# Band matrices made whole, statistics row by row, squares in longer pieces and fewer filler matmuls in a two-branch image kernel

## The reference

```python
def reference(x, ln_w, ln_b, q_w, q_dw, kv_w, kv_dw, proj_w, temperature, w1, w3, w5, wd, wf):
    x = x + attention(_gn(x), ...)       # L0
    x = x + convolutions(_gn(x), ...)    # L1
    return x

def _gn(v, G=32, eps=1e-05):             # group norm, 3 channels a group, no weights
    g = v.reshape(B_, G, C_ // G, H_, W_)
    m = jnp.mean(g, axis=(2, 3, 4), keepdims=True)
    s = jnp.var(g, axis=(2, 3, 4), keepdims=True)
    return ((g - m) / jnp.sqrt(s + eps)).reshape(v.shape)

# attention: xn = layer norm over channels; q = dwconv3x3(conv1x1(xn, q_w), q_dw); kv likewise;
#   k, v = split(kv); q, k normed along the pixels; softmax(q k^T * temperature) v; conv1x1(., proj_w)
# convolutions: x1 = 1x1, x2 = 3x3, x3 = 5x5, x4 = 3x3 dilated by 2; conv1x1(concat(x1..x4), wf)
```

## Time and profile before

| | us |
|---|---|
| median of 3 runs (lowest, highest) | 1850.2 (1848.76, 1851.78) |
| the profiled execution: its time | 1848.9 |
| its span | 1847.2 |
| PE busy | 1754.8 (95%) |
| DVE busy | 1517.0 (82%) |
| ACT busy | 1024.4 (55%) |
| POOL busy | 516.1 (28%) |

### The profile page before, as it was taken

One profiled execution on the slowest core, in us unless ns is written; L12 is line 12 of the kernel. 1 busy time (PEld: TensorE's weight loads), 2 busy tenths in 40 slices (PEclk: granted clock), 3 DMA queues, 4 the chain that ended last, 5 costly groups with the idle time before them and its releaser, 6 DMA issues.

```text
span 1847.2 us, 43054 instructions
## 1 busy us (share of the span) xinstructions
PE 1754.8 (95%) x14228; PEld 1678.0 (91%) x14228; DVE 1517.0 (82%) x2182; ACT 1024.4 (55%) x1736; POOL 516.1 (28%) x347
## 2 busy tenths in 40 slices
PE   4999999999999999999999999999999999999998
PEld 3889878999989996999999997889998999699998
DVE  4799868999877657999968665899996865689997
ACT  0756556555285746655437663755536665665451
POOL 5599500232272000123238000022325400003222
PEclk9999989999999998999999999899999999899999
DMA  7012203566501200566630210166661121035553
GB/s 192 0 35 68 63 1 78 149 173 169 159 18 51 75 11 1 122 168 177 171 107 13 68 55 1 36 156 167 175 165 44 36 71 30 1 81 153 131 143 99
DMA packets 101476, 166.83 MB, mean 90 GB/s; under 512 B 40040, under 2 KB 74568, under 8 KB 101224
## 3 DMA queue, kind: packets, MB, share of 16 engines
q1 hardware_dynamic: 76040, 136.91, 29.3%
q10 hardware_dynamic: 25344, 28.75, 4.8%
HBM read 52.86 MB, written 25.17 MB: 42 GB/s over the span
## 4 chain that ended last, share of the span: by engine, by line
PE 73%; issue 8%; DVE 7%; ACT 4%; DMA 2%; POOL 1%; ACTq 1%; SPq 1%; DVEq 1%; POOLq 0%
PE ps L802 35%; PE ps L661 11%; PE ps L704 6%; PE ps L680 6%; PE ps L682 6%; PE ps L681 6%; DVE region L1208 3%; ACT region L948 2%; PE ps L635 2%; DMA X<-in_x_dram 1%; POOL region L560 1%; PE ps L797 1%; PE ps L733 1%; DMA region<-region 1%; PE ps L691 0%
## 5 line engine op out<-in xcount | busy, mean ns | idle before, releaser
L802 PE MATMUL ps<-region,W 128*96 128x256 f16 (+4 forms) x7156 | 803.9, 272 | 10.9 <-ACT region L976 10.5
L802 PEld LDWEIGHTS ps<-region,W 128*96 128x96 f16 (+2 forms) x7156 | 781.2, 122 | 25.1 <-issue 19.6
L570 POOL TENSOR_TENSOR region<-region 96x528 f32<-96x528 f32 (+1 forms) x72 | 96.4, 1344 | 1013.1 <-ACT region L962 689.4
L1208 DVE TENSOR_TENSOR region<-V,band 128x387 f32<-128x387 f32 (+2 forms) x288 | 298.3, 1098 | 82.9 <-PE ps L682 81.4
L981 ACT ACTIVATE region<-region 96x1584 f16<-96x1584 f32 (+2 forms) x88 | 110.8, 1301 | 329.6 <-DVE region L1298 308.5
L680 PE MATMUL ps<-region 128*128 x1152 | 225.7, 278 | 9.4 <-DVE region L1208 8.8
L682 PE MATMUL ps<-region 128*128 x1152 | 222.7, 275 | 0.0
L681 PE MATMUL ps<-region 128*128 x1152 | 222.2, 274 | 0.0
L1384 DVE SCALAR_TENSOR_TENSOR region<-ps,small,region 96x768 f32<-96x768 f32 (+1 forms) x220 | 203.7, 988 | 14.2 <-PE ps L802 12.9
L661 PE MATMUL ps<-proj,region 96*128 96x240 f32 x1024 | 212.9, 372 | 0.0
L661 PEld LDWEIGHTS ps<-proj,region 96*128 96x128 f32 x1024 | 197.9, 194 | 14.0
(11 more groups left out here) (169 smaller groups left out, 2170.7 us busy)
## 6 DMA issues: line engine op xcount, KB each, us to landing
region<-region SPq DMA_DIRECT2D x108, 247.5 KB, 4.0
region<-in_x_dram SPq DMA_DIRECT2D x128, 192.0 KB, 2.4
out_dram<-region SPq DMA_DIRECT2D x40, 576.0 KB, 4.2
region<-region ACTq DMA_DIRECT2D x80, 247.5 KB, 2.4
X<-in_x_dram SPq DMA_DIRECT2D x30, 576.0 KB, 6.0
region<-region SPq DMA_DIRECT2D x36, 247.4 KB, 4.9
X<-in_x_dram SPq DMA_DIRECT2D x19, 384.0 KB, 14.8
region<-region SPq DMA_DIRECT2D x24, 185.6 KB, 3.6
```

The source lines that it names most:

```text
L802: last = mm(o, w, src, start=k == 0, stop=k == len(steps) - 1, skip_group_check=split and ck > 0)
L1208: v.tensor_tensor(T[:, i, 3 * c:3 * c + m].rearrange("p m (i j) -> p m i j", j=3), taps.broadcast_to([P, m, BW // 3, 3]), mask.broadcast_t ...
```

## The change

There are four edits.

- *Band matrices.* From the second chunk of each image on, one operation of 2322 elements makes a chunk's 18 matrices and raises `s_T` by 3. The first chunk keeps its three operations. The first pair of chunks stands ahead of the loop, which now begins at the second pair.
- *First image's statistics.* Each of the 16 loads has a semaphore of its own. DVE's 32 `bn_stats` are written out without a loop, each load's two behind a wait for that load: 12 loads ahead of the search for the largest weight, two behind line 1107, one behind line 1111, the last behind line 1119 and ahead of the seven scalings.
- *Squares.* Seven sets are squared in one piece of 2048 each, in a loop; the last set follows outside the loop in two pieces of 1024. There is one scratch buffer, and every piece waits until the one before it has finished.
- *Fillers.* 40 instead of 64 filler products ahead of unit 0.

```diff
-        tsums = sb("tsums", [C, AT + AT // 2])
+        tsums = sb("tsums", [C, AT + AT // 4 + 1])
...
-        junk = [work[0:C, a:a + BANK].bitcast(bf16) for a in (900, 900 + BANK)]
+        junk = work[0:C, 900:900 + 2 * BANK].bitcast(bf16)
...
-        s_first = [plain_sem("first_rows_loaded%d" % k) for k in range(LS // UG)]
+        s_first = [plain_sem("first_rows_loaded%d" % k) for k in range(LS)]
...
-                keep_warm(0, 64)
+                keep_warm(0, 40)
...
-                with act.Fori(0, SETS) as k:
+                def squared(k, half, parts, n):
+                    width = 4 * BANK // parts
+                    act.wait_ge(s_xs, b * (SETS + 1) + n + START)
+                    act.activation(junk[:, 0:width], X[:, bass.ds(k * 4 * BANK + half * width, width)], ACT.Square,
+                                   bias=col(MEAN), scale=-1.0, accum_out=tsums[:, bass.ds(AT + n, 1)]).then_inc(s_xs, 1)
+                with act.Fori(0, SETS - 1) as k:
                     act.wait_ge(s_x1, (b * SETS + k + 1) * AR + START)
-                    for u in range(2):
-                        act.wait_ge(s_xs, (b * SETS + k) * 2 + u - 1 + START)
-                        act.activation(junk[u], X[:, bass.ds((k * 2 + u) * 2 * BANK, 2 * BANK)], ACT.Square,
-                                       bias=col(MEAN), scale=-1.0,
-                                       accum_out=tsums[:, bass.ds(AT + k * 2 + u, 1)]).then_inc(s_xs, 1)
+                    squared(k, 0, 1, k)
+                act.wait_ge(s_x1, (b + 1) * SETS * AR + START)
+                for half in range(2):
+                    squared(SETS - 1, half, 2, SETS - 1 + half)
...
+            def statistics(first, end):
+                for m in range(first, end):
+                    dve.wait_ge(s_first[m], 16)
+                    for t in range(m * XL, m * XL + XL):
+                        v.bn_stats(stats[:, t, :], X[:, t * BANK:(t + 1) * BANK]).then_inc(s_bn, 1)
+            statistics(0, 12)
...
-                with dve.Fori(0, DK // 2) as k2:
+                def bands(k2, i, parts):
...
+                    for c, channels in parts:
+                        m = 3 * channels
+                        taps = V[:, :, bass.ds((k2 * 2 + i) * DM + 3 * c, m)].rearrange("p j m -> p m j").unsqueeze(2)
+                        v.tensor_tensor(T[:, i, 3 * c:3 * c + m].rearrange("p m (i j) -> p m i j", j=3),
+                                        taps.broadcast_to([P, m, BW // 3, 3]), mask.broadcast_to([P, m, BW // 3, 3]),
+                                        ALU.mult).then_inc(s_T, len(PARTS_OF_T) // len(parts))
+                WHOLE = ((0, DC),)
+                bands(0, 0, PARTS_OF_T)
+                bands(0, 1, WHOLE)
+                with dve.Fori(1, DK // 2) as k2:
                     for i in range(2):
...
+                        bands(k2, i, WHOLE)
```

More of the change, by code:

```diff
@@ L372, in _ @@
                 sync.dma_start(X[:, m * LR * W:(m + 1) * LR * W],
-                               x[0:1, :, m * LR:(m + 1) * LR, :].rearrange("o c h w -> (o c) (h w)")).then_inc(s_first[m // UG], 16)
+                               x[0:1, :, m * LR:(m + 1) * LR, :].rearrange("o c h w -> (o c) (h w)")).then_inc(s_first[m], 16)
             def stage_rows(b, c, j, free):
@@ L1108, in _ @@
             assert setup.n == N_AMAX
+            statistics(12, 14)
             dve.wait_ge(s_pt, 15)
@@ L1112, in _ @@
             assert setup.n == N_GMAX
+            statistics(14, 15)
             dve.wait_ge(s_pt, 16)
@@ L1120, in _ @@
             assert setup.n == N_WSC
+            statistics(15, LS)
             for at, factor in OSCS:
                 link(setup, v.tensor_scalar(col(at), col(POW), factor / (WTOP * YSCALE), None, ALU.mult))
-            first_statistics(LS // UG - 1)
             NEXT_AT = 500
@@ L1194, in _ @@
                     scaled(AT - AD + i, i, i == AD - 1)
-                with dve.Fori(0, DK // 2) as k2:
-                    for i in range(2):
[L1200 to L1210, removed]
+                def bands(k2, i, parts):
+                    n = b * DK + k2 * 2 + i
+                    dve.wait_ge(s_dw, n - 1 + START)
+                    dve.wait_ge(s_out, b * UNITS * 16 + START)
+                    dve.wait_ge(s_pq, (b + 1) * AT + START)
+                    dve.wait_ge(s_V, N_TURNED)
+                    mask = band[:].rearrange("p (i j) -> p i j", j=3).unsqueeze(1)
+                    for c, channels in parts:
[8 more added lines that the diff above has]
+                with dve.Fori(1, DK // 2) as k2:
+                    for i in range(2):
+                        bands(k2, i, WHOLE)
                 dve.wait_ge(s_qd, (b + 1) * DK + START)
@@ L1261, in _ @@
                 assert st.n == N_MEAN2
-                dve.wait_ge(s_xs, (b + 1) * AT // 2 + START)
+                dve.wait_ge(s_xs, (b + 1) * (SETS + 1) + START)
                 squares_of(st, tsums)
```

## The result

| | before | after |
|---|---|---|
| median of 9 runs of each, side by side (lowest, highest) | 1850.15 (1848.1, 1852.5) | 1842.18 (1838.92, 1846.11) |
| the profiled execution: its time | 1848.9 | 1841.69 |

A forecast was written before the change was run, and what follows sets the result against it. PE bounds the depthwise stage, except in the first image, where DVE and POOL take turns at the port; ACT's chain sets the seams. Terms -9.2 + 0.5 + 0.9 - 1.4 + 0.6 + 0 = -8.6 gave 1841.6 us; range 1838 to 1847.

The forecast's parts named there:

- Band matrices, -9.2: First image's depthwise stage: one operation meets at most one POOL turn, so PE becomes the bound; 9.2 us less, bounds 4 and 10.2.
- Only part comes back: Rival: turns fall badly and leftovers hold up the first image's Gram stage; 1846 to 1848 us, chance 0.13.
- Second chunk, +0.3: Depthwise stage, images 2 to 4: whole operation exposes handover and slower first matmul; 0.3 us more an image, 0.9 in all.
- POOL's leftovers, +0.5: First image's Gram stage: 8 to 12 POOL operations move there and meet DVE's copies; 0.5 us more, bounds 0 and 3.
- Statistics, -1.4: First image's setup: DVE keeps up with the loads, so ACT's folding and PE's 24 filler records start earlier; 1.4 us less.
- a case that the prediction named: Setup: if the cold clock holds for longer in the 24 filler records, the statistics give only 1.1 us.
- Squares, +0.6: Last set of squares: second piece waits for the first's accumulator; 0.15 us more an image, bounds -0.1 and +0.3.
- Fillers, 0: Ahead of unit 0: it starts 3.6 us earlier, but unit 1 still waits for ACT's last copy; 0 us in all.
- the slower rival: Units 0 and 1: fewer fillers bring clock drops, 1.5 to 1.7 us lost at each; 1855 us, chance 0.04.
- the sign that I had named: Wait for ACT's last copy grows from 10.5 to about 17 us; if it stays or goes, the prediction is wrong.

## Why the prediction was right

*Band matrices, -9.2: right, measured -9.06 with the stage's start.* PE became the bound, as the sum had it. The mechanism was confirmed from the other side too: with POOL silent the old operations give 97.10. The mean wait for a turn was 0.50 (0.36 against an undisturbed operation), where I took 0.65 and "at most one turn"; the turn of 2.43 was worked out to 0.03. The Trainium skill (SBUF — State Buffer, "SBUF: two separate sides") is borne out by the operation at 123.48.

*Only part comes back* (the first rival) is out: the first image's depthwise stretch is 98.7, within 1.5 of the others'.

*Second chunk, +0.3: right in size, by two numbers.* The stage itself is 0.43 longer; its first product comes 0.11 earlier, since the first chunks now stand outside the loop (argued, not shown). The copy of the second chunk came 4.44 after that of the first, 567.51 against 563.07, instead of 576.93 - 572.91 = 4.02. With three parts for the second chunk again the 0.43 vanished.

*POOL's leftovers, +0.5: the mechanism right, the size too small.* I had 8 to 12 operations in the Gram stage with the question open whether one-input copies wait for POOL. 15 remained, and POOL's split ended at 233.51, 21 us behind the depthwise stretch's end instead of 8 to 12, perhaps because DVE's wider operations also hold POOL back for longer (argued, not shown). And the copies do wait: 1215 ns instead of 993, as this timeline shows (DVE, then POOL):

```profile
228.19 1.01 DVE L1225 COPY region<-region 128x960 f32 x1 [0.69 <-PE ps L704]
230.09 1.54 DVE L1225 COPY region<-region 128x960 f32 x1 [0.88 <-PE ps L704]
231.99 3.15 DVE L1225 COPY region<-region 128x960 f32 x2 [0.35 <-PE ps L704]
...
228.28 2.44 POOL L522 TENSOR_TENSOR W<-region,W 96x768 f16<-96x768 f32 x1
230.78 2.73 POOL L538 MEMSET W<- 128x2208 f16 x1
```

The copy of 228.19 began 0.09 ahead of POOL's L522 and took 1.01, no longer than with POOL silent, and L522 ended 1.52 after it. That of 230.09 met the end of L522 and took 1.54. The two of 231.99, met by a memset that reads nothing, took 3.15 together. The term is 1.03 at full clock, within its bounds of 0 and 3.

*Statistics, -1.4: right in kind, too large.* 1.18 and 0.41 in the pairs with nearly equal landing. The first pair of profiles read 1.65, with the last rows landed 43.40 - 42.38 = 1.02 later in the kernel before. What I had not allowed for is this scatter. The lower value goes with longer fillers (5.38 for the 24 records), a case that the prediction named but took for -1.1. That it is the clock is not shown.

*Squares, +0.6: wrong, measured -0.04 an image.* The later second piece (+0.12) was as forecast. I took the gain of leaving the loop as "up to 0.1"; it was 0.17, the start 0.12 instead of 0.29 behind the end of DVE's last addition.

*Fillers, 0: right for the path to unit 1, not shown for the whole time.* Unit 0 started 3.4 earlier (forecast 3.6), except in the third image, whose fillers had run at full clock before (14.54 for all 128 records instead of 16.17). PE stood 3.38, 1.77 and 2.02 ahead of it in the first three images, where I had 1.7. The gain was gone by unit 1. Alone, the edit came out 3 us slower, and no trace ties that to the fillers. The wait for ACT's last copy grew from 10.5 to 12.0, not to 17: the rest stands in the waits for DMAs, 12.4 in total, because unit 0's third point waits too, and because 3.4 us at or near 1.2 GHz at unit 0's start eat a part:

```profile
285.40:289.00 3.60, 0.77 (x6) 0.75 (x7) 3.53 (x4) 0.17 (x1) 0.00 (x0) 0.95 0.65 142
289.00:292.40 3.40, 3.40 (x19) 3.19 (x18) 2.69 (x2) 3.40 (x3) 0.00 (x0) 0.55 0.21 43
292.40:295.80 3.40, 3.40 (x33) 3.40 (x32) 3.21 (x4) 3.40 (x3) 0.00 (x0) 1.00 0.12 28
```

PE did 0.77 of work in 3.60, and then 19 products in 3.40 instead of 33. This is the clock drop that the slower rival named; the price per drop was right, and the wait behind it hides it: unit 1 starts 0.06 later than before, counted from the group mean. With the fillers changed alone the wait for ACT's last copy was 10.2 and that for DMAs 15.4, while unit 1 stayed where it was. So the sign that I had named, a wait that stays at 10.5, doesn't show whether the path is as I had it; both waits have to be counted.

That the sum came within 0.6 of the measured 8.0 owes something to luck. The leftovers were taken 0.5 too small and the squares some 0.8 too large, and these two largely cancel; both are smaller than the scatter of single runs.

*What stays open.* Why the stage that adds to `X` grew by 0.38 in every image when the statistics were changed alone; and what makes PE stand 3 to 4.5 us at some image starts, with "issue" as the only cause shown. In the changed kernel it is this one:

```profile
1388.98 1.22 PE L635 MATMUL ps<-ident 128*128 128x128 f32 x4 [3.67 <-issue]
```

This stall, 1.4 longer than in the kernel before, stands in the 2.5 us by which the first profile missed the sum of the table, and a longer stretch at the lower clock may be the rest. Stretches of 3.4 us at the lower clock also come in one execution and not in another. That stalls and stretches are what spreads the runs of one kernel over 2 to 11 us is argued, not shown. The repeat of the changed kernel, without that stall, took 1838.61, 3.1 less, but its setup was 1.2 and its last Gram stage 1.5 shorter too.

## What to carry to other kernels

Where two engines took turns here, what cost was the number of turns: the same 2322 elements in one operation instead of three met POOL at most once instead of up to three times, DVE's waiting fell from 1.64 to 0.36 a chunk, and 9 us came back with the same products on PE. Look at what the other engine does with its share: work that it couldn't finish moves into the next stage and meets new operations there. Before an edit on filler work is credited or blamed, find the wait that comes after it: 3.4 us ahead of unit 0 and a clock at half moved unit 1 by less than 0.5, because ACT's chain set its time. And compare profiles stage by stage only where the granted clock is the same: the same Gram stage takes 28.87 or 30.5 with the clock alone.

## What the runs showed of the hardware

- PE at the start of an image usually stands 1.8 to 2.6 us; in some executions 3.4 to 4.5 with no releaser in the profile (4.50, 3.67, 3.39; the longest with 64 fillers was 3.15). These are too few executions to tie it to an edit.
- The last of the first image's rows landed between 40.0 and 44.1, with the same 16 loads in every kernel.
